# Normalising the rows between two graph layers on GpSimd instead of VectorE

## The reference

```python
h = relu(layernorm(x))                       # (x - mean) / sqrt(var + eps), per row
msg = where(type == 0, h[src] @ Wd.T + bd, h[src] @ Wc.T + bc)
x = x + relu(segment_sum(msg, dst) + h @ Ws.T + bs)
h = relu(layernorm(x))                       # the rows this change is about
e = (tanh(h[dst] @ gd + h[src] @ gs + b) + tanh(yn)) * 0.5 * d[dst] * d[src]
x = x + segment_sum(h[src] * e, dst)         # d = max(degree, 1) ** -0.5
```

## Time and profile before

| what | value |
|---|---|
| time, median of 3 runs | 6099.6 us (6097.68 to 6100.94) |
| span of the profiled execution, first to last instruction | 6092.6 us |
| busy: GpSimd, VectorE, TensorE, ScalarE | 4501.2, 4228.4, 4187.7, 2756.7 us |
| chain that ended last | GpSimd's line L569 71%, issue 23% |

### The profile page before, as it was taken

The page is one execution under the profiler, slowest core; times in us unless marked ns, Lnnn a source line. Parts: engine busy times, 40 slices in busy tenths (PEclk is TensorE's granted clock), DMA queues, the critical chain, the costliest instruction groups (busy, mean ns, idle before and its releaser), DMA issues.

```text
span 6092.6 us, 113200 instructions
## 1 busy us (share of the span) xinstructions
PE 4187.7 (69%) x28031; PEld 3131.0 (51%) x28031; DVE 4228.4 (69%) x15670; ACT 2756.7 (45%) x9511; POOL 4501.2 (74%) x4524
## 2 busy tenths in 40 slices
PE   6577777777777777765566666666666666666754
PEld 5355555555555555543455555555555555555543
DVE  6877777777777777755366767777776767676763
ACT  5555555555555555533144444444444444444430
POOL 5777777777777777777547777777777777777774
PEclk8588898888989888987688888888888887887775
DMA  7766666666666666666354444444444444444434
GB/s 239 237 198 195 198 191 199 194 194 198 197 193 198 195 192 199 195 199 199 89 135 110 110 111 107 111 110 110 109 111 109 111 110 109 108 110 109 109 95 114
DMA packets 714900, 930.26 MB, mean 153 GB/s; under 512 B 132464, under 2 KB 525716, under 8 KB 713748
## 3 DMA queue, kind: packets, MB, share of 16 engines
q1 hardware_dynamic: 562819, 622.14, 34.5%
q0 software_dynamic: 142848, 297.41, 18.8%
q10 hardware_dynamic: 8592, 3.46, 0.2%
HBM read 862.14 MB, written 60.37 MB: 151 GB/s over the span
## 4 chain that ended last, share of the span: by engine, by line
POOL 71%; issue 23%; PE 2%; DVE 2%; DMA 2%; ACT 0%; SPq 0%; DVEq 0%; ACTq 0%; POOLq 0%
POOL G L569 71%; PE PS L882 1%; PE PS L890 0%; DMA OWF<-in_x 0%; DMA HTB<-ini 0%; DMA G<-t,IDXB 0%; DMA out<-OWF 0%; DVE ST L1169 0%; PE PS L877 0%; DVE OHF L1180 0%; SPq L311 0%; DVE OWF L1188 0%; DVE G L1641 0%; DVE ACC L1487 0%; DVE ACC L1483 0%
## 5 line engine op out<-in xcount | busy, mean ns | idle before, releaser
L569 POOL DMA_INDIRECT G<-t,IDX x4256 | 4216.1, 991 | 1350.2 <-issue 1297.6
L1080 PE MATMUL PS<-CDST,HTB 128*128 128x256 f32 x2092 | 821.2, 481 | 270.7 <-DVE CDST L1770 242.0
L704 ACT ACTIVATE OHF<-PS 128x384 bf16<-128x384 f32 x1568 | 768.5, 490 | 455.3 <-PE PS L926 434.8
L938 PE MATMUL PS<-CDST,OHF 128*128 128x256 bf16 x4704 | 837.4, 291 | 14.4 <-DVE ACC L1280 13.5
L1071 PE MATMUL PS<-HTB,OWF 128*128 128x129 f32 x3136 | 792.2, 341 | 9.1 <-DVE OWF L1749 9.1
L1071 PEld LDWEIGHTS PS<-HTB,OWF 128*128 128x128 f32 x3136 | 689.5, 238 | 170.0 <-issue 87.0
L796 ACT ACTIVATE ST<-PS,MV 128x1 f32<-128x1 f32 x1568 | 407.2, 260 | 581.3 <-issue 237.0
L938 PEld LDWEIGHTS PS<-CDST,OHF 128*128 128x128 bf16 x4704 | 491.6, 105 | 294.5 <-issue 80.3
L899 PE MATMUL PS<-G,OHF 128*32 128x128 f32 x4256 | 219.2, 335 | 600.0 <-DMA G<-t,IDX 553.0
L1080 PEld LDWEIGHTS PS<-CDST,HTB 128*128 128x128 f32 x2092 | 400.7, 238 | 349.9 <-ACT HTB L815 320.4
L899 PE MATMUL PS<-G,OWF 128*32 128x128 f32 x4256 | 227.7, 347 | 481.5 <-DVE OWF L1731 481.5
(11 more groups left out here) (239 smaller groups left out, 8916.7 us busy)
## 6 DMA issues: line engine op xcount, KB each, us to landing
HTB<-t0s SPq DMA_DIRECT2D x392, 384.0 KB
OWF<-t0s SPq DMA_DIRECT2D x392, 384.0 KB
HTB<-t SPq DMA_DIRECT2D x784, 132.0 KB
G<-t,IDX POOLq DMA_INDIRECT x4256
YN<-rows SPq DMA_DIRECT2D x784, 64.0 KB
OHF<-rows SPq DMA_DIRECT2D x784, 64.0 KB
t0s<-HTB SPq DMA_DIRECT2D x25, 384.0 KB
t0s<-OWF SPq DMA_DIRECT2D x24, 384.0 KB
```

The costliest lines, as they stand in the source:

```text
L569: eng.indirect_dma_start(out=G[:, k:k + width], out_offset=None, in_=table, in_offset=bass.IndirectOffsetOnAxis(ap=at, axis=0)).then_inc(s ...
L704: eng.activation(X0[:, k % KX, :, :].rearrange("p n w -> p (n w)"), PS[:, cell_bank(k), 0:384], ACT.Identity).then_inc(q_ev, 1)
L938: ins = eng.matmul(PS[:, 4, 0:DW], X0[:, k % KX, n, :], CD0[:, k % KD, :], start=b == 0 and n == 0, stop=b == NB - 1 and n == 2)
L1080: eng.matmul(PS[:, 4 + g % 2, 0:DW], X1[k % KX1], CD1[k // 2 % 3][:, k % 2, :], start=b == 0, stop=b == NB - 1).then_inc(d_ap, 1)
```

## The change

The seven `tensor_scalar` instructions of a chunk move from VectorE to GpSimd. VectorE keeps the reciprocal of the deviations, and signals it with a new semaphore, `b_rs`. GpSimd waits for it, and for `HN`'s two readers, normalises, and signals `a_n`. In GpSimd's list the norm of chunk c-1 stands ahead of the memset of chunk c. The memset of `XB` moves one round earlier in that list, to stand behind the norm of chunk 10.

```diff
@@ gpsimd, between the layers
-            for c in range(NC):
-                if c == NC - 2:
+            for c in range(NC + 1):
+                if c >= 1:
+                    d = c - 1
+                    eng.wait_ge(b_rs, d + 1)
+                    if d >= 2:
+                        eng.wait_ge(b_t2, d - 1)
+                        eng.wait_ge(b_hd, d - 1)
+                    for i in range(CB):
+                        b = d * CB + i
+                        ins = eng.tensor_scalar(HN[d % 2][:, i, :], X1B[d % 2][:, i, :], MV[:, b, 0:1], RS[:, b:b + 1],
+                                                ALU.subtract, ALU.mult)
+                    ins.then_inc(a_n, 1)
+                if c == NC - 3:
 
                     eng.wait_ge(b_x1, NC - 2)
                     eng.memset(XB[1][:, CB - 1, :], 0.0).then_inc(s_xz, 1)
-                eng.wait_ge(b_t, c + 1)
-                eng.memset(ACC[:, 0, c * CB * 128:(c + 1) * CB * 128], 0.0).then_inc(s_z, 1)
+                if c < NC:
+                    eng.wait_ge(b_t, c + 1)
+                    eng.memset(ACC[:, 0, c * CB * 128:(c + 1) * CB * 128], 0.0).then_inc(s_z, 1)
@@ vector
-            def norm(c, X, to):
+            def deviations(c):
                 eng.wait_ge(a_sq, NC + c + 1)
-                link(eng.reciprocal(RS[:, c * CB:(c + 1) * CB], SQ[:, c * CB:(c + 1) * CB]))
-                for i in range(CB):
-                    b = c * CB + i
-                    ins = eng.tensor_scalar(to[:, i, :], X[:, i, :], MV[:, b, 0:1], RS[:, b:b + 1],
-                                            ALU.subtract, ALU.mult)
-                ins.then_inc(a_n, 1)
+                eng.reciprocal(RS[:, c * CB:(c + 1) * CB], SQ[:, c * CB:(c + 1) * CB]).then_inc(b_rs, 1)
...
                     degrees(c - 1)
-                    if c >= 3:
-
-                        eng.wait_ge(b_t2, c - 2)
-                        eng.wait_ge(b_hd, c - 2)
-                    norm(c - 1, X1B[(c - 1) % 2], HN[(c - 1) % 2])
+                    deviations(c - 1)
```

More of the change, by code:

```diff
@@ L275, in gnn_program @@
         b_dm, b_dg, b_ds, b_d, b_idx = sems("b_dm", "b_dg", "b_ds", "b_d", "b_idx")
-        b_t, b_x1, b_hd, b_t2, b_pd = sems("b_t", "b_x1", "b_hd", "b_t2", "b_pd")
+        b_t, b_x1, b_hd, b_t2, b_pd, b_rs = sems("b_t", "b_x1", "b_hd", "b_t2", "b_pd", "b_rs")
         c_x, c_s = a_x[0:5], a_x[5:8]
```

## The result

| | before | after |
|---|---|---|
| time, median | 6100.0 us (6097.7 to 6100.9, 4 runs) | 6153.4 us (6149.6 to 6158.2, 4 runs) |
| ratio | 1 | 1.0084, 95% interval 1.007 to 1.0098 |
| span of the profiled execution | 6092.6 us | 6152.8 us |
| first new_x to first gather of layer 1 | 105.9 us | 148.4 us |
| first gather of layer 1 to the end | 2986.6 us | 3000.1 us |

The change makes the kernel 53 us slower, 0.84%, where 9.5 were forecast and 26 was the high end. The spans differ by 60.2 us: 42.4 in the changed stage, 13.5 in layer 1, whose code is untouched, and 4.2 ahead of the stage, where later runs of both kinds of kernel lie anywhere between 2998 and 3009 us. The profiled execution of after took 6154.65 us, 1.85 more than its span.

What follows compares the result with a forecast made beforehand. GpSimd's gather queue bounds the kernel, VectorE the changed stage. Rounds +7.9, tail +1.3 and XB memset +0.3 give +9.5 us on the 6092.6 span, 6102.1; with 7.0 to the median, 6109.1 us, range 6093 to 6126.

Steps and rivals of the forecast that it cites:

- the high end: GpSimd's seven norms at 4.5 us, with another fixed part each for fetching scalars; gives +26 us, 6126.
- the serial line: Stage between layers: new_x, stats, reciprocal, norm, new_x stay in one line, since new_x(c) waits for chunk c-2's norm.
- my formula: A round: 3.62 us new_x through reciprocal, 0.06 handover, norm 3.2, 0.10 handover back; 6.98 us, twelve rounds +7.9.
- Added on GpSimd: Cost of 98 norm instructions moved to GpSimd, bounded by its int32 rows; 3.2 us per seven, ends 1.7 and 4.5.
- N: Time of a chunk's seven norm instructions on GpSimd, taken as 3.2 us; the sum is 13 N - 32.1.
- the overlap of 0.06: Back-to-back GpSimd instructions overlap by about 0.06 us, read from two memsets of 0.20 us starting 0.14 apart.
- the slow form: GpSimd's one-operation int32 rows: 2.54 ns a column and 0.19 us fixed, 0.51 us for 128 columns.
- The fast form: GpSimd's two-operation int32 row: 0.83 ns a column, 0.30 us an instruction, seven in 1.7; underlies rival B, chance 0.23.
- The tail: End of the stage: TensorE waits for norm 12, 3.26 us after the reciprocal instead of 1.92; +1.3 us.
- The memset of XB: Moved behind norm 10, it makes a later load land 14.2 us after new_x, needed at 13.96; +0.3 us.
- rival C: Contention: a VectorE instruction can stand behind a whole GpSimd one; under 1 us expected; within something else, 0.03.
- Rival A: At new_x's wait for a_n, the norm becomes the loop's long part; 13 us per us of N, slower; chance 0.38.

Runs made afterwards that it cites:

- e2: Changed kernel with the two per-partition scalars of GpSimd's norm replaced by constants 0.0 and 1.0; 6139.7 us, one run.
- e7: Changed kernel with each GpSimd norm instruction over 64 of its 128 columns; 6145.2 us, one run.
- e8: Kernel before, with the memset of ACC waiting for new_x of its chunk instead of its transposes; 6099.1 us, ratio 0.9997.
- e11: Changed kernel with the norm shared, VectorE doing blocks 0 to 4 and GpSimd 5 and 6; 6109.2 us, ratio 1.0019.
- e14: Changed kernel with a one-column copy on GpSimd behind its last memset of the stage; 6141.7 us, one run.
- e12: Kernel before plus 8 one-column tensor_scalar instructions on GpSimd between the layers; 6110.2 us, one run.
- e10: Kernel before plus 84 one-column tensor_scalar instructions on GpSimd between the layers; 6117.1 us, ratio 1.0026.
- e15: Shared norm of e11 with e14's copy and a third buffer of x, loaded three chunks ahead; 6091.1 us, ratio 0.9979 to the kernel before.
- e13: Kernel before plus 84 one-column copies on GpSimd between the layers; 6104.5 us, one run.
- e4: Kernel before plus 84 one-column memsets on GpSimd between the layers; 6097.4 us, one run.
- e3: Kernel before plus one 128x16 tensor_scalar with two per-partition scalars on GpSimd between the layers; 6096.2 us, one run.

## Why the prediction was wrong, point by point

- **The point on which I rested, the serial line: right.** VectorE waited 68.1 us for GpSimd, in front of twelve of the fourteen new_x. A round is 3.62 + 0.06 + 5.44 + 0.10 = 9.22 us by my formula and 9.25 in the trace; twelve are 111.1 us, by the formula 110.6. No load of x was late, as said. The memset of ACC beside new_x cost nothing, as said: from new_x to the end of the reciprocal it is 3.58 us, where it was 3.62.
- **The step that failed is "Added on GpSimd".** I took N = 3.2 us with 4.5 as the end; it is 5.44. At 13 us for each us that alone is +29 us. By e2 and e7 the fixed part (0.18 us) was right. The column costs 3.4 ns and not the 2.54 of the int32 rows: 0.10 us an instruction. The two scalars cost 0.16 us, which I had named, counted in the high end as 0.19, and left out of the value taken. And the overlap of 0.06 that I subtracted, read from memsets, is not there beside the fixed 0.18, which is counted from start to start. 0.45 + 0.10 + 0.16 + 0.06 = 0.77. Even the high end was low, because it added only one unknown to the slow form and held its slope and the overlap for safe.
- **The fast form** (one two-operation row, 1015 ns for 992 columns) did not hold for subtract and mult on fp32. I gave the cases that need it 0.23.
- **The Trainium skill's** GPSIMD Engine Reference, section 4.1, has one-input operations roughly at line rate, and section 8 VectorE twice as fast. The trace has 0.78 us against VectorE's 0.27, 2.9 times. Both rules put GpSimd's time too low, and the measurement decides.
- **The tail: +7.3 us for +1.3.** From the last new_x to the transposes of HN 12 it is 9.17 us where it was 5.60 (+3.6, by N as above). Norm 13 was not under the 5.49 us between the transposes: the memset and seven norms are 6.2 us (+0.7). From there to the first gather it is 18.80 where it was 15.83 (+3.0). The three products of chunk 12 took 5.75 us at a granted clock of 0.53 (3134.95 to 3140.70), near the 1.2 GHz level, where before they took 3.21 us at 1.00, the 2.4 GHz level (3091.58 to 3094.79); the last store of the table also landed 0.6 us more slowly (3.67 us for 3.11). TensorE had stood for 3.74 us ahead of them; that this is what lowered the clock is not shown. I had seen the clock as a price of a longer round; in the rounds it cost nothing, since every wait of new_x ended on GpSimd, and in the tail it did.
- **The memset of XB: 0 for +0.3.** The longer rounds gave the load its time.
- **Contention (rival C): not where I put it.** The memset and VectorE's norm do collide (e8), tensor_scalar on both hardly does (e11).
- **Layer 1: +13.5 us, in no part of the prediction.** I wrote that a microsecond won in the stage is one of the total and that the change touches neither edge stage. It does, by the 7 ns of each gather: without them (e14) layer 1 is back in the range of the kernel before, and over all traces they are worth 10 to 12 us of the 13.5.
- **One reading of the rows was loose.** I put the 0.2 us by which the mean round of before lies above 6.13 down to late loads. The loads held VectorE for 3.6 us, 0.3 a round; against them stand the first two of the twelve rounds, of 5.60 and 5.63 us, whose norms met no memset. The sum uses the whole 75.9 us and is not touched.
- **The sum, redone with what was measured:** 13 x 5.44 - 32.1 = 38.6 in place of 9.5; with 3.7 us more of tail and 13.5 of layer 1 it is 55.8, on a median of 6099.6 that makes 6155, against 6153.4. Two of its terms are the measured ones, so this closes the books and tests nothing. Rival A was the right case, with its price far short: its high end added 26 us, the change 53.

## What to carry to other kernels

Before work is moved to an idle engine, follow the buffer that it frees: if the first engine's next instruction waits for that buffer, the work stays in the same line, and the move wins only where the second engine is about as fast at it. Price an instruction by its parts, fixed, scalars and columns, and when no row of its kind exists let the high end stack all unknowns at once. And look at what the engine does afterwards: here 13.5 of the 60.2 us were lost in GpSimd's gathers, in a stage that the change did not touch.

## What the runs showed of the hardware that I had not expected

- With 8, 28, 84 or 98 tensor_scalar instructions on GpSimd (e12, e11, e10, after), the 2232 indirect DMAs behind them took 7 ns more (947 in place of 940 ns at least), for thousands of us; with one copy of one column behind them (0.19 us) they did not (e14, e15). Copies and memsets in number do not bring it (e13, e4), nor did one tensor_scalar (e3); most of these are single runs.
- An fp32 tensor_scalar of 128 x 128 with two per-partition scalars takes 0.78 us on GpSimd: 0.18 fixed, 0.16 for the scalars, 3.4 ns a column. On VectorE it takes 0.27.
- A GpSimd memset of 896 columns beside VectorE's seven norms made them 0.46 us longer (2.34 to 1.89 without it, e8); two of GpSimd's tensor_scalars beside five of them added about 0.13 (e11).
